# A two-layer interaction kernel: two product groups of layer 1 in three reduced-precision passes, with gathers and products in other places

## The reference

```python
e = jnp.stack([tbl_f[ids[:, f]] for f in range(32)], axis=1)   # 512 x 32 fields x 32
for W in (filter_0, filter_1):                                  # 128 maps each
    z = jnp.einsum('bhd,bmd->bhmd', x0, prev)                   # every field by every map
    cur = relu(jnp.einsum('bpd,pn->bnd', z.reshape(b, h * m, d), W[0]))
    prev = cur
h = concat([sum over d of both layers' cur, dense_ctx])         # 512 x 272
h = relu(h @ W_top1 + b_top1); h = relu(h @ W_top2 + b_top2); y = h @ W_top3
```

## Time and profile before

| | before |
|---|---|
| median of 3 runs | 938.97 us (935.41 to 939.64) |
| the profiled execution's own time | 945.5 us |
| its span, first to last instruction | 943.6 us |
| PE busy | 880.3 us (93%) |
| DVE busy | 743.9 us (79%) |
| POOL busy | 716.2 us (76%) |
| ACT busy | 655.2 us (69%) |
| mean granted clock of PE | 0.993 |

### The profile page before, as it was taken

The page is one execution under the profiler, slowest core; times in us unless marked ns, Lnnn a source line. Parts: engine busy times, 40 slices in busy tenths (PEclk is TensorE's granted clock), DMA queues, the critical chain, the costliest instruction groups (busy, mean ns, idle before and its releaser), DMA issues.

```text
span 943.6 us, 17792 instructions
## 1 busy us (share of the span) xinstructions
PE 880.3 (93%) x3519; PEld 660.3 (70%) x3519; DVE 743.9 (79%) x2328; ACT 655.2 (69%) x2199; POOL 716.2 (76%) x834
## 2 busy tenths in 40 slices
PE   2989979999999999999999999999999999999998
PEld 1567757777777777767777777777777767767774
DVE  2498857897777788777779877777987777898893
ACT  2567747777766777776677777677777767777772
POOL 5167869877888887787888778788877878787780
PEclk9999999999999999999999999999999999999998
DMA  6756666557676656766765676675567667555430
GB/s 178 209 114 154 152 142 143 117 136 160 147 159 156 134 117 141 162 146 155 161 130 114 147 164 146 152 164 128 116 147 163 147 147 161 124 123 146 90 67 1
DMA packets 55480, 131.16 MB, mean 139 GB/s; under 512 B 8100, under 2 KB 19332, under 8 KB 55461
## 3 DMA queue, kind: packets, MB, share of 16 engines
q0 software_dynamic: 22240, 68.17, 40.7%
q1 hardware_dynamic: 31538, 59.99, 20.2%
q10 hardware_dynamic: 1683, 2.80, 0.9%
HBM read 60.67 MB, written 4.20 MB: 69 GB/s over the span
## 4 chain that ended last, share of the span: by engine, by line
PE 35%; POOL 20%; DMA 18%; issue 18%; DVE 3%; SPq 2%; ACT 2%; POOLq 1%; DVEq 0%; ACTq 0%
DMA x_shift<-x_rows 10%; POOL prod L293 9%; POOL emb L252 6%; PE t_dve L710 5%; PE t_act L710 5%; PE t_act L712 5%; PE t_act L711 5%; PE t_dve L712 5%; PE t_dve L711 5%; DMA x_rows<-emb 5%; DMA emb<-table_dram,row_ids 4%; POOL prod L275 4%; PE acc L683 3%; ACT prod L402 2%; DVE prod L542 1%
## 5 line engine op out<-in xcount | busy, mean ns | idle before, releaser
L402 ACT ACTIVATE prod<-t_act,weigh 128x128 f32<-128x128 f32 x2048 | 580.5, 371 | 195.8 <-PE t_act L712 194.0
L542 DVE SCALAR_TENSOR_TENSOR prod<-t_dve,weigh,prod 128x128 f32<-128x128 f32 x1792 | 473.5, 335 | 1.1 <-DVE prod L542 0.5
L293 POOL TENSOR_TENSOR prod<-prod 128x512 f32<-128x512 f32 (+1 forms) x255 | 333.2, 1307 | 10.4
L710 PE MATMUL t_dve<-w_hi,cur_hi 128*128 128x512 f32 x512 | 204.0, 399 | 39.9 <-DVE prod L542 39.9
L494 DVE TENSOR_TENSOR z<-x_shift,x_same 128x1024 f32<-128x1024 f32 x64 | 100.3, 1568 | 162.6 <-DMA x_shift<-x_rows 162.6
L710 PE MATMUL t_act<-w_hi,cur_hi 128*128 128x512 f32 x512 | 216.4, 423 | 0.1
L712 PE MATMUL t_act<-w_hi,cur_lo 128*128 128x512 f32 x512 | 201.1, 393 | 0.0
L711 PE MATMUL t_act<-w_lo,cur_hi 128*128 128x512 f32 x512 | 200.5, 392 | 0.0
L712 PE MATMUL t_dve<-w_hi,cur_lo 128*128 128x512 f32 x512 | 200.4, 391 | 0.0
L711 PE MATMUL t_dve<-w_lo,cur_hi 128*128 128x512 f32 x512 | 200.2, 391 | 0.0
L252 POOL DMA_INDIRECT emb<-table_dram,row_ids x128 | 133.6, 1044 | 39.7 <-issue 38.9
(11 more groups left out here) (77 smaller groups left out, 456.1 us busy)
## 6 DMA issues: line engine op xcount, KB each, us to landing
prod<-prod POOLq DMA_DIRECT2D x126, 512.0 KB, 4.7
x_shift<-x_rows SPq DMA_DIRECT2D x64, 512.0 KB, 6.2
x_pair<-x_rows SPq DMA_DIRECT2D x96, 128.0 KB, 5.3
x_same<-x_rows SPq DMA_DIRECT2D x32, 256.0 KB, 5.2
x_rows<-emb SPq DMA_DIRECT2D x64, 64.0 KB
w_raw<-w_dram ACTq DMA_DIRECT2D x8, 256.0 KB, 4.2
emb<-table_dram,row_ids POOLq DMA_INDIRECT x128, 3.7
w_raw<-wt_dram SPq DMA_DIRECT2D x2, 512.0 KB, 5.4
```

Of the source, the lines that this page charges most:

```text
L293: nc.gpsimd.tensor_tensor(src[:, dst, :], src[:, dst, :], src[:, other, :], ALU.add).then_inc(folded, 1)
L402: last = nc.scalar.activation(prod[i][:, HEADS * k + j, :], t_act[k % ARING][:, j * MAPS:(j + 1) * MAPS], ACT.Copy, scale=weigh[p][:, i, h ...
L542: nc.vector.scalar_tensor_tensor(dst, src, w, dst, ALU.mult, ALU.add).then_inc(added, 1)
L710: nc.tensor.matmul(bank[:, :], cur_hi[p][:, cols], w_hi[:, w], start=True, stop=False)
```

## The change

Groups 2 and 3 of layer 1 (`SPLIT` = 2 of them, behind the first `WHOLE` = 2) are no longer plain float32 matmuls for chunks 1 to 31. Weights and products are split into a high and a low float32r part, and each group is done in three passes. The high part of the products (`z_hi`) comes from ACT, the low part (`z_lo`) from DVE; the weights are split once, by DVE, at the start. Chunk 0's layer 1 stays as it is. Further, POOL's gathers stand two after tile 0 and two after tile 1, and on DVE products 0 stands after tile 1, and `place` goes from behind tile 2 to behind tile 0.

```diff
+        z_hi = sb("z_hi", [128, SPLIT, COLS], f32r)
+        z_lo = sb("z_lo", [128, SPLIT, COLS], f32r)
+        v_hi = sb("v_hi", [128, SPLIT, MAPS], f32r)
+        v_lo = sb("v_lo", [128, SPLIT, MAPS], f32r)
...
-                        gather((p + LEAD) % 2, ((0,), (1,), (2, 3), ())[i])
+                        gather((p + LEAD) % 2, ((0, 1), (2, 3), (), ())[i])
...
+            def round_pair(c, p):
+                act.wait_ge(z_ready, c * 3 + 3)
+                act.wait_ge(layer1_done, c)
+                nc.scalar.activation(z_hi[:, :, :], z[p][:, WHOLE:GROUPS, :], ACT.Copy).then_inc(pair_rounded, 1)
...
                     weigh_tile(c, i, p)
+                    if i == 0 and not (isinstance(c, int) and c + 1 >= CHUNKS):
+                        round_pair(c + 1, 1 - p)
...
+            def lower_pair(c, p):
+                dve.wait_ge(pair_rounded, c)
+                for k in range(SPLIT):
+                    nc.vector.tensor_tensor(z_lo[:, k, :], z[p][:, WHOLE + k, :], z_hi[:, k, :].bitcast(fp32),
+                                            ALU.subtract).then_inc(z_lo_ready, 1)
...
+            dve.wait_ge(v_ready, 1)
+            nc.vector.tensor_copy(v_hi[:, :, :], v[:, WHOLE:GROUPS, :]).then_inc(v_ready, 1)
+            dve.wait_ge(v_ready, 2)
+            nc.vector.tensor_tensor(v_lo[:, :, :], v[:, WHOLE:GROUPS, :], v_hi[:, :, :].bitcast(fp32),
+                                    ALU.subtract).then_inc(v_ready, 1)
...
                 add_tile(c, 0, p)
+                if more1:
+                    lower_pair(c + 1, 1 - p)
+                place(c, p)
+                add_tile(c, 1, p)
                 if more2:
                     products(c + 2, p, 0)
-                add_tile(c, 1, p)
-                if more2:
                     products(c + 2, p, 2)
                 add_tile(c, 2, p)
                 if more1:
                     lower(c + 1, 1 - p)
                     pooling1(c + 1, 1 - p)
-                place(c, p)
...
-                    if g < GROUPS:
+                    if g < WHOLE:
                         if g == 0:
                             pe.wait_ge(z_ready, c * 3 + 1)
-                        elif g == WHOLE:
-                            pe.wait_ge(z_ready, c * 3 + 3)
                         nc.tensor.matmul(acc1[:, :], v[:, g, :], z[p][:, g, :], start=g == 0, stop=False)
+                    elif g < GROUPS:
+                        k = g - WHOLE
+                        pe.wait_ge(z_lo_ready, (c - 1) * SPLIT + k + 1)
+                        for weights, rows in ((v_hi, z_hi), (v_lo, z_hi), (v_hi, z_lo)):
+                            nc.tensor.matmul(acc1[:, :], weights[:, k, :], rows[:, k, :], start=False, stop=False)
```

More of the change, by code:

```diff
@@ L135, in dlrm_tower @@
         z_rounded = sem("z_rounded")
+        pair_rounded, z_lo_ready = sem("pair_rounded"), sem("z_lo_ready")
         z_parts_ready = sem("z_parts_ready")
@@ L576, in _ @@
             nc.vector.tensor_tensor(v[:, :, :], v[:, :, :], v_b[:, :, :], ALU.add).then_inc(v_ready, 1)
+            dve.wait_ge(v_ready, 1)
[3 more added lines that the diff above has]
+                                    ALU.subtract).then_inc(v_ready, 1)
             nc.vector.tensor_copy(v_parts[:, :], v_last[:, :]).then_inc(v_ready, 1)
             low = slice(2 * FIELDS, 3 * FIELDS)
-            dve.wait_ge(v_ready, 1 + 1)
+            dve.wait_ge(v_ready, 1 + 3)
             nc.vector.tensor_tensor(v_parts[low, :], v_last[low, :], v_parts[low, :].bitcast(fp32),
@@ L737, in _ @@
             warm_up(WARM_UPS, t_dve[DRING - 1])
-            pe.wait_ge(v_ready, 1 + 2)
+            pe.wait_ge(v_ready, 1 + 4)
             first_layer1()
```

## The result

The changed kernel takes 881.62 us (median of 4 runs, 878.33 to 883.09); the kernel before took 938.49 us beside it. The ratio is 0.9394, with a 95% interval of 0.9359 to 0.9429. The forecast was 884 us. The profiled execution has a span of 879.3 us; that of the kernel before had 943.6.

The account below looks back on a forecast made before the run. The gather-write-read loop was taken to bound the kernel, PE next at 25.85 us a chunk. Terms of -55.0, -4.6 and -0.3 us take the span from 943.6 to 883.7; forecast 884 us, range 875 to 903.

Parts of the forecast that it names:

- The loop: Gathers, SP's write, `x_shift` read, DVE's product, tile 1 and POOL's tick: 27.58 us a chunk; opening it gains 49 us.
- last link: From `x_shift` landing to DVE's `z` product, which starts at 494.43 and ends at 496.39.
- PE's floor: PE's own matmul time with small waits: 26.2 us a chunk before, 25.85 us after the change.
- The passes: Layer 1 on PE: six float32r passes replace four float32 records, -0.35 us a chunk, 11 us in all.
- Rival 2: The six new passes on PE cost as float32 ones: 27.05 us a chunk, 920 us; chance 0.03.
- `round_pair`, `lower_pair`, `place`: ACT's copy, DVE's subtractions and selection behind tile 0: price 0; uncovered, up to 1.3 us (copy) or 1.4 us (DVE).
- POOL's room: POOL needs 24.5 us a chunk, 1.4 us under PE, its work hardly changed by the new order.
- the lock: DVE instructions with two SBUF inputs and POOL instructions reading SBUF exclude each other for their whole length.
- Rival 1: DVE or POOL leaves PE a smaller wait, 0.5 to 1.0 us a chunk: 899 to 914 us; chance 0.12.
- rival 4: POOL becomes the bound, running in turn with DVE's two-input work: 28.5 us a chunk, 961 us; chance 0.04.
- The ends: Outside the 29 chunks: first chunk 26.4 us (-4.6), chunk 0's own passes -0.3, last 60.8 us unchanged.
- the two cases that the forecast left open: Profiled execution's excess: a slow chunk the new slack hides, 885.6 us for the runs, or not, 879.

Follow-up runs that it names:

- the fill: Kernel before, with a fill of 1536 unused columns on POOL behind the first gather of each chunk: ratio 0.9887.
- The run with more work on PE: Changed kernel with the three passes of group 2 done twice each chunk: 26.48 us a chunk, ratio 0.9686.
- the run with less work on PE: Changed kernel with group 1 left out of layer 1 in chunks 1 to 31: 25.49 us a chunk, ratio 0.933.

## Why the prediction was right, and where it was not

**The loop.** Right in length and in what opens it. Either move alone removes the wait of DVE and of PE. Wrong in its last link: I took the product's 1.96 us as its price and the landing at 494.43 as what released it. POOL's add of 493.99 held it; the fill, which delays that add, made most chunks shorter with the transfers as they were. The loop that I had drawn is there too, but second in length: with its own 1.22 us the product of 494.43 would have ended 0.74 us earlier, which gives 26.8 us a chunk, and half of the chunks with the fill take about that, 26.6 to 27.1, while DVE still waits some 5 us for `x_shift`. The error cost the forecast nothing, and that was luck in part: both chains begin with the tick of tile 1, and the new places are 8 us clear of both.

**PE's floor.** 26.2 - 0.35 = 25.85 us was forecast and 25.80 measured, with 26.15 in the run without the split. I had put 0.2 us of small waits on PE's 25.96 us; there are 0.19. The run with more work on PE shows that it is PE which sets the chunk.

**The passes.** 0.35 us forecast, 26.15 - 25.80 = 0.35 measured; -11 us in all. Rival 2 is out by the run with three passes more.

**`round_pair`, `lower_pair`, `place`.** Price 0 on the path, and 0 it is: the copy takes 1.07 us, DVE waits 0.22 us for it, and doing the subtractions twice costs at most 0.06 us. What I did not see is that the subtractions have a price elsewhere. In the old places they cost 28.27 - 27.60 = 0.7 us a chunk through POOL's adds. In the changed kernel they fall beside POOL too, but POOL is no longer in the loop.

**POOL's room.** Forecast 24.5 us of 25.85. Here the forecast failed: POOL shows no wait in the middle chunks. Its four ticks took 0.58 + 3 x 0.20 = 1.18 us before, and take 0.54 + 0.65 + 0.20 + 1.11 = 2.50 now; in the same chunk its `side` adds are 1.0 us longer in sum, and its large adds 1.2 us shorter. I had taken POOL's 24.5 us over unchanged, with no term for what the new order does to the lock. It did not decide: the run with less work on PE still reached 25.49, and with product 0 behind tile 0 POOL had waits again at the same 25.80. Rival 1 and rival 4 name this mechanism; it begins 0.3 us under PE's time, not 1.4.

**The ends.** From relu1 of chunk 2 to that of chunk 31: forecast 749.7, measured 748.1 us. From relu1 of chunk 1 to that of chunk 2: 26.4 against 27.27; there `z_last` waited 3.2 us for x. Up to relu1 of chunk 1: 46.85 against 46.23. The end: 60.8 against 57.7 us. The sum of these is the 4.4 us between 883.7 and 879.3. The 3.1 us at the end are PE's clock, which the change was not expected to touch. The kernel before, in the stretches of the dense tower, has:

```profile
924.00:928.00 4.00, 4.00 (x11) 1.40 (x12) 1.38 (x2) 0.60 (x1) 0.00 (x0) 0.83 0.02 4
928.00:932.00 4.00, 4.00 (x10) 3.13 (x11) 0.00 (x0) 0.69 (x1) 0.00 (x0) 0.50 0.01 2
932.00:936.00 4.00, 4.00 (x16) 3.17 (x15) 3.79 (x6) 3.00 (x5) 0.00 (x0) 0.82 0.00 0
```

The granted clock is 0.50 of full there, the lower of the two levels (1.2 of 2.4 GHz), after a stretch (920 to 924) in which PE was busy 3.43 of 4 us; the changed kernel had 3.46 of 4 in the like stretch and kept its clock. This differs from one execution to the next, and is no part of the change: of the 14 profiled executions, 7 have a granted clock of 1.00 in the end and take 57.6 to 58.2 us for it, 7 have 0.94 to 0.97 and take 59.2 to 60.8, and kernels near to the one before and near to the changed one are in both groups. So 3.1 of the 64.3 us between the two spans go with the clock and not with the change.

Of the two cases that the forecast left open for the 6.5 us by which the profiled execution before exceeded the runs' median, the first came: the profiled execution now takes 881.15 us and the median is 881.62.

## What to carry to other kernels

When every chunk has the same length to a few hundredths and no engine is busy all the time, follow the loop until it closes, and take PE's own sum of passes as the floor. Then check each link's length against its usual length: an instruction that lasts longer than elsewhere hides a wait that no list of waits shows. Here it was POOL's add before DVE's product, and a fill of 1.4 us that delayed the add made most chunks shorter.

Work that is free in an engine's idle time can still cost, if it holds something that a third engine needs.

## What the runs showed of the hardware that I had not expected

A DVE product with two SBUF inputs that had stood waiting for a transfer, and started 0.23 us before a POOL add, still waited for the add (496.75 and 496.98). By the trace's start times the bound lies between 0.75 us, the longest lead with which such a product was held, and 0.79, the shortest with which it went first, both in the run with the fill. Where the product followed other DVE work without a wait, a lead of 0.16 us could be enough: in the changed kernel it starts at 472.96 and takes 1.21 us, and POOL's tick of 473.12 takes 1.11. It was not always enough: the product of 290.80 in the run with double subtractions had a lead of 0.35 us and was held for 3.10. What sets this bound is not shown, and the profile's times on POOL are rough. A product that met two adds in a row waited for both: 3.08 us for a product of 1.22. Beside the fill itself it did not wait.
